# Where the two parts of the attention maxima are made: on GpSimd ahead of the loads, instead of on VectorE

## The reference

```python
q = split_heads(layernorm(x) @ wq); k = split_heads(ctx @ wk); v = split_heads(ctx @ wv)
scores = jnp.einsum('bhqd,bhkd->bhqk', q, k) / 4          # 8 batches, 16 heads, 512 x 512
x = x + tanh(gate) * (einsum('bhqk,bhkd->bhqd', softmax(scores), v) merged @ wo)
```

## Time and profile before

| | |
|---|---|
| median of 3 runs | 1637.36 us (1636.45 to 1640.37) |
| profiled execution | 1638.76 us, its span 1636.8 us |
| TensorE busy | 1461.8 us, 89% |
| VectorE busy | 1287.1 us, 79% |
| ScalarE busy | 1012.0 us, 62% |
| GpSimd busy | 637.2 us, 39% |
| attention, layer 0 | about 114 to 430 us of the span |
| attention, layer 1 | about 1205 to 1525 us |

### The profile page before, as it was taken

How to read it: one execution, slowest core, us unless ns; L and a number is a source line. 1 busy time by engine, 2 the same in 40 slices (tenths; PEclk the granted TensorE clock), 3 DMA queues, 4 the chain that set the end, 5 groups by cost and what they waited for, 6 DMA issues and landing times. The chain is left out here.

```text
span 1636.8 us, 29399 instructions
## 1 busy us (share of the span) xinstructions
PE 1461.8 (89%) x10910; PEld 952.2 (58%) x10910; DVE 1287.1 (79%) x2140; ACT 1012.0 (62%) x1750; POOL 637.2 (39%) x957
## 2 busy tenths in 40 slices
PE   7989999999994399999999999869979999999846
PEld 6853333333483299999999999745533333333534
DVE  6889999999575766666665564379889999999687
ACT  5648999999642144444444444335549999999544
POOL 4315555556031234344442332255425555553120
PEclk9989999999995599999999999979979999999976
DMA  9975555555262122222222221168845555554103
GB/s 288 331 207 110 128 127 129 127 126 127 85 234 87 45 62 90 73 84 94 68 81 91 73 80 36 45 197 291 245 93 125 127 124 128 127 126 103 34 0 103
DMA packets 118748, 198.64 MB, mean 121 GB/s; under 512 B 29568, under 2 KB 63680, under 8 KB 117584
## 3 DMA queue, kind: packets, MB, share of 16 engines
q1 hardware_dynamic: 83840, 111.22, 22.3%
q0 software_dynamic: 33360, 83.94, 20.5%
q10 hardware_dynamic: 1408, 1.61, 0.3%
HBM read 117.77 MB, written 77.87 MB: 120 GB/s over the span
## 5 line engine op out<-in xcount | busy, mean ns | idle before, releaser
L1141 ACT ACTIVATE i_room<-a_ring 128x512 f32<-128x512 f32 x1024 | 550.5, 605 | 61.2 <-PE a_ring L1077 13.8
L349 DVE TENSOR_REDUCE logit<-a_ring 128x2 f32<-128x1024 f32 x416 | 488.3, 1217 | 3.5 <-PE a_ring L343 3.5
L1088 PE MATMUL a_pout<-i_room,values 128*17 128x256 f32 x4096 | 309.4, 386 | 3.3 <-ACT i_room L1141 1.8
L1779 ACT ACTIVATE e_full<-e_pH,b1T 128x320 f32<-128x320 f32 x256 | 135.0, 527 | 246.6 <-PE e_pH L1720 235.8
L1728 PE MATMUL e_pY<-fc_w,e_hid_hi 128*128 128x512 f32 x640 | 237.2, 407 | 0.5 <-DVE e_hid_lo L1832 0.5
L1077 PE MATMUL a_ring<-i_qk 64*128 64x512 f32 x768 | 193.9, 503 | 19.0 <-DVE logit L349 16.3
L1729 PE MATMUL e_pY<-fc_w,e_hid_lo 128*128 128x256 f32 x640 | 179.9, 281 | 0.0
L1077 PEld LDWEIGHTS a_ring<-i_qk 64*128 64x128 f32 x768 | 72.6, 186 | 182.9 <-DVE logit L349 134.2
L1088 PEld LDWEIGHTS a_pout<-i_room,values 128*17 128x17 f32 x4096 | 74.7, 96 | 175.7 <-ACT i_room L1141 136.9
L1840 POOL DMA_INDIRECT w<-normed,slot_get x80 | 84.1, 1052 | 225.7 <-PE fc_turned L1705 199.5
L1832 DVE TENSOR_TENSOR e_hid_lo<-e_full,e_hid_hi 128x640 fp32r<-128x640 f32 x128 | 119.6, 934 | 55.7 <-ACT e_hid_hi L1788 55.7
(11 more groups left out here) (335 smaller groups left out, 2583.4 us busy)
## 6 DMA issues: line engine op xcount, KB each, us to landing
ks<-i_room SPq DMA_DIRECT2D x64, 256.0 KB, 4.1
outs<-a_osb SPq DMA_DIRECT2D x64, 256.0 KB, 3.4
qs<-i_room SPq DMA_DIRECT2D x60, 256.0 KB, 5.2
fc_raw<-in_L_ffn_fc_w SPq DMA_DIRECT2D x15, 1024.0 KB, 5.3
i_qk<-ks POOLq DMA_DIRECT2D x84, 128.0 KB, 3.4
i_qk<-qs POOLq DMA_DIRECT2D x84, 128.0 KB, 3.6
BIG<-outs SPq DMA_DIRECT2D x64, 128.0 KB
ytok<-r_zeros SPq DMA_DIRECT2D x8, 1024.0 KB, 10.3
```

Source lines behind the costliest of these rows:

```text
L349: return e.tensor_reduce(nmax[:, :].rearrange("p (x y t) -> p x y t", x=2, y=2)[:, :, p, t], pair[:, :, :], AX.X, ALU.max, negate=True)
L1088: mm = e.matmul(pout[32 * h:32 * h + VW, at], v[:, b * TPB + t, g * HG + h, :], pexp[t][:, h, at], start=(t == 0 and half == 0), stop=(t = ...
L1141: e.activation(pexp[t][:, 2 * p + hh, :], score_bank(n * U + i, hh), ACT.Exp).then_inc(exped, 1)
L1779: e.activation(full[s % 2][:, h * WIDE:(h + 1) * WIDE], pH[h][:, 0:WIDE], ACT.Silu, bias=S.b1T[:, n * KF + f:n * KF + f + 1]).then_inc(act, 1)
```

## The change

The two instructions that make `nparts` leave VectorE's `turn_maxima` and become `cut_maxima(n)` on GpSimd. In GpSimd's loop it stands ahead of a load, and the load's place moves by one iteration: where GpSimd did `load(n + 4)` it now does `cut_maxima(n + 1)` and then `load(n + 3)`. What each load itself waits for (`scored`) is unchanged. `cut_maxima(n)` waits for the reductions of group n, and for the transposition of group n - 2, whose parts it overwrites. On VectorE the transposition of group n no longer follows its last reduction at once: it stands one reduction later, behind the first of group n + 1, and waits for `cut`. For the last group it follows the last reduction.

```diff
+TURN_LAG = 1
@@ GpSimd
+                def cut_maxima(n):
+                    halves, whole = max_halves(nparts[n % 2]), max_whole(nmax[n % 2])
+                    if n >= 3:
+                        e.wait_ge(nturned, n - 2)
+                    e.wait_ge(reduced, (n + 1) * U - AHEAD)
+                    e.tensor_copy(halves[:, :, 0, :], whole).then_inc(cut, 1)
+                    e.wait_ge(cut, 2 * n - 1)
+                    e.tensor_tensor(halves[:, :, 1, :], whole, halves[:, :, 0, :], ALU.subtract).then_inc(cut, 1)
+
@@
                 for n in range(NG):
-                    if n + G < NG:
-                        load(n + G)
+                    if n + 1 < NG:
+                        cut_maxima(n + 1)
+                    if 0 < n <= NG - G:
+                        load(n - 1 + G)
                     if l == 0 and n % G == 1:
@@ VectorE
                 def turn_maxima(n):
-                    halves, whole = max_halves(nparts[n % 2]), max_whole(nmax[n % 2])
-                    e.wait_ge(reduced, (n + 1) * U - AHEAD)
-                    e.tensor_copy(halves[:, :, 0, :], whole).then_inc(cut, 1)
-                    e.wait_ge(cut, 2 * n - 1)
-                    e.tensor_tensor(halves[:, :, 1, :], whole, halves[:, :, 0, :], ALU.subtract).then_inc(cut, 1)
                     if n >= 3:
                         e.wait_ge(mrow[(n - 2) % G], moved(n - 2))
                     e.wait_ge(cut, 2 * n)
@@
                     reduce(m)
-                    if m % U == U - 1:
-                        turn_maxima(m // U)
+                    if m % U == TURN_LAG - 1 and m >= 2 * U:
+                        turn_maxima(m // U - 1)
+                turn_maxima(NG - 1)
```

## The result

The changed kernel takes 1706.03 us in the median (1700.43 to 1711.76) against 1637.09 of the kernel before, a ratio of 1.0412 with a 95% interval of 1.0395 to 1.0429. It is 69 us slower; the forecast was 1645 in a range of 1620 to 1672. The profiled execution, at 1700.43 us the shortest of the four, has a span of 1698.7 us, 61.9 more than before. The transpositions place it. In layer 0 thirty of them lay 292.5 us apart before (130.3 to 422.8) and lie 326.1 apart now; in layer 1, 31 lay 305.2 apart (1209.1 to 1514.3) and now 334.0. That is 33.6 + 28.8 = 62.4 us, the whole difference.

What follows compares the result with a forecast made beforehand. VectorE's turn was taken to bound each group, with TensorE's work next. Floor 9.75 plus load wait 0.5 gave 10.25 us a group: +9.5 over 56 groups, -2.0 over six, +7.5 us on 1637.36, so 1645, range 1620 to 1672.

Steps and rivals of the forecast that it cites:

- The turn leaves the path: VectorE's 0.73 us between groups' reductions makes TensorE's fourth score unit wait 0.38 us; the change removes that wait.
- The floor of 9.75 us: An attention group takes TensorE's own 9.70 us plus 0.05 allowed, 0.34 below now; over 62 turns 21 us.
- GpSimd's parts, 0.68 us: Two 16-element operations plus hops on GpSimd: the next load is issued 0.68 us after the last reduction.
- The lock: Rival: the cut waits behind GpSimd's or VectorE's shared ports, 1.17 us each; 1678 us, chance 0.05.
- The load starts 3.11 us later: Behind the cut, a load starts at 261.62 instead of 258.51, using 3.11 us of a 2.99 us slack.
- c = 0.5 us of contention: A load's end lands 0.5 us later because its busiest stretch meets output stores and fetches; bounds -0.5 and 1.3.
- the forecast's own 0.2 to 0.9: Range of c, the load's later landing, under which the forecast case gives 1638 to 1656 us, chance 0.42.
- the prediction's own sign, a time past 10 us: Load time from issue to landing growing past 10 us would show the forecast wrong, with 1661 us and more.
- The moves of the maxima, nothing: Moves after the transposition start about 0.7 us later but just fit before the next group's scores; nothing charged, upper end 0.9 a group.
- Half of the lateness is paid: At TensorE's unit i = 1, a load 1.01 us late costs a wait of 0.5 us each group.
- my 10.25: Forecast group time in us: 9.75 floor plus 0.5 wait for the load, 0.16 to 0.17 more than now.
- The third rival: Load, moves and store fill the DMA engines together, c 1.1 or more: 1661 us, up to 1685; chance 0.17.

Runs made afterwards that it cites:

- the changed kernel without its loads: Changed kernel with eight of a load's ten DMAs left out for groups 4 to 31: 1634.9 us, 0.9968 of the kernel before.
- the split ones: Changed kernel with the first five DMAs of a load issued ahead of the cut, five behind: 1635.43 us, 0.9975; timed again 1635.20 us, 0.9977.
- the old order without loads: Kernel before with eight of a load's ten DMAs left out: 1642.3 us, 1.0022 of the kernel before.
- Late loads alone: Kernel before, parts still on VectorE, but GpSimd waits for the group's parts ahead of the load: 1714.6 us, 1.0451.
- The small stores: Changed kernel with SyncE storing and fetching back only 64 of 512 columns of each group's output: 1675.55 us, 1.0205 of the kernel before.

## Why the prediction was wrong

**The turn leaves the path: right.** The matmuls' 10.6 us of waiting for VectorE in 27 groups are gone, and the transposition waits in only two of 62 groups, 1.5 us in all. But the wait for ScalarE that took its place is nearly as long, 0.29 us a group against 0.39.

**The floor of 9.75 us: wrong, it is 10.01.** The step took TensorE's work without its wait, 9.70, as the next bound, and compared the other engines by their busy sums. What came next was no engine's sum but a loop: score, exponential, and the bank that the exponential frees, 1.2 us long, at the one unit without values. It lay 0.08 us behind the turn (10.01 against 10.09 us a group) and needed no change to appear. Of 21 us, 4 to 5 are left (the changed kernel without its loads, and with the split ones). And most of these aren't the turn's own length: the prediction read the cast's 0.25 us as its cost, where 0.17 is its cost and 0.08 comes of the load that GpSimd issues beside it. Where that load is missing, the old order runs at 10.01 to 10.03 as well. No experiment took the cast alone out of the load's way with the rest left in place; this rests on the comparison of groups.

**GpSimd's parts, 0.68 us: right.** They took 0.69. The lock never closed in the changed kernel: all 62 casts lie between 192 and 199 ns. The Trainium skill's exemption of tensor_reduce (SBUF — State Buffer, Who interferes with whom) holds here, beside reductions from PSUM.
```profile
L1051 POOL CAST logit<-logit x62: 192/196/199, 119.1 to 1576.8; 128x16 fp32r<-128x16 f32 x62
```
The other way round it did close, in the old order without loads: VectorE's cast of 0.17 us took up to 1.12 beside GpSimd's addition. That the change takes this cast off VectorE was a merit that the prediction didn't name.

**The load starts 3.11 us later: right, and the mechanism of the loss.** Late loads alone gave 1714.6.

**c = 0.5 us of contention: mis-sized where it counts.** The 14 loads of layer 0 that TensorE waited for took 10.5 us in the mean; against the 8.9 of before that is a c of 1.6. The 14 not waited for took 9.0, a c of 0.1. The mean of all, 0.8, is within the forecast's own 0.2 to 0.9; but only the waited ones count, and for them the prediction's own sign, a time past 10 us, was fulfilled. I took one value for all from a load of which only the last two issues met a store. The small stores show that part of it is the stores; what the rest is (the maxima's moves, the load's own queue) wasn't separated.

**The moves of the maxima, nothing: nearly right.** From 140 to 420 TensorE's matmuls waited for them three times, 1.6 us in all.

**Half of the lateness is paid: right as a mean, wrong as a picture.** I assumed a steady 0.5 us in each group. A load's start hangs on the reduction of the unit made at i = 0, one unit ahead of the place where TensorE waits. So the wait of a group doesn't put off the next load, only the one after it: a load ties a group to the one before the last, and nothing evens out neighbours. They fall apart: one group waits, by up to 2.2 us, the next not at all. The pairing may also feed on contention, though no run tests this apart. In the two loads shown, the one that starts in a group without a wait has moves and stores right behind it (SyncE's moves at 288.68, 0.7 us after the load's start at 287.94) and lands late; the one that starts while TensorE waits has them 3 us later (277.60 against 274.18) and lands early.

**The clock: not in the sum.** Waits as short as forecast would have left it alone: with the small stores, whose waits for loads are at most 0.9 us from 140 to 420, it stays at 1.00. In the changed kernel it fell to the lower level for a stretch after a single wait of 2.12 us, and the group that shows it lost 4.06 - 2.59 = 1.5 us more. That isn't so after every wait: of the eight waits of 1.6 to 2.2 us in layer 0 at six the clock fell, and at the two that ended at 252.91 and 436.21 (1.99 and 1.96 us) it didn't. The changed kernel's clock is 0.96 over 280 us, the mean at half the level being about 8% of that time. With five stretches in layer 1 there are eleven, at 1.5 us each some 17 us of the loss. That is an estimate; no run takes the clock apart, since with the small stores shorter landings come with it.

**The sum with these sizes.** From a waited product to the next waited one, two groups on, it is the floor, 10.01, then 1.14 to the next load's first issue (264.17 - 263.03), then 10.5 of load and 0.13 of wake (by the load of 264.17, landed at 275.19): 21.8 for two groups, 10.9 for one. Eleven stretches of the clock in some 28 pairs add 0.3: 11.2, where 11.13 and 11.24 were measured. From my 10.25 the floor adds 0.13, the landing of the waited loads 0.58 and the clock 0.3, over 56 groups 7, 32 and 17 us. So the landing time is the term that failed most. This sum is worked out, not measured part by part. The third rival had the mechanism, contention that decides from c = 0.9, but priced it at 1661 to 1685 with the same floor and no clock, and the range cut it off at 1672.

## What to carry to other kernels

Before an instruction is put ahead of a DMA issue in a queue, compare what it waits for with what the DMA waits for: here the load's start moved from one event to another 2.4 us later, and the wait for it, not the two small operations of 0.2 us behind it, cost 69 us: with the wait alone the loss was there in full. Splitting the queue's own work around the new instruction kept the operations and avoided the loss. Where an instruction takes longer in its place than the same one elsewhere (0.25 us against 0.17), ask what runs beside it before its whole length is counted as a gain; and look over a control run for costs of its own, as the one without loads had. Where a stall is to be removed, look for the loops between two engines through a shared buffer at that very place, not only for the engines' sums. And where a late transfer ties a group to the one before the last, expect the waits in every other group at double size, and price what a long idle does to the clock.

## What the runs showed of the hardware

A single idle of TensorE of 2.12 us was followed by a stretch at the lower clock (0.50 from 275.2 to 278.6), in which 16 matmuls took 1.91 us instead of 1.06. Between the kernel before, the small stores and the changed kernel the median landing of a load's DMA stayed at 3.4 to 3.5 us while the longest went from 4.6 to 5.6 and 7.1: the tail grew and the middle stayed. The last two differ in the size of the stores and fetches. A GpSimd cast of 128x16 took 0.20 us and a subtraction 0.22, and a hop between VectorE and GpSimd 0.1. VectorE's cast of the same 16 elements took 174 to 176 ns with no GpSimd work beside it, 185 to 268 in the 56 groups with one, and 1.06 to 1.12 us in eight groups beside a GpSimd addition of 128x1024.
